# An attention layer on one core: scores and values' products in 64-row halves in one stretch, and the totals of the group norm in the values' bank

## The reference

```python
# group norm: 16 groups along the last axis of x, over (C, H, W/16)
m = mean(g); s = var(g); xn = (g - m) / sqrt(s + 1e-5)
# windows: 8 x 8 pixels, a 4 x 4 grid of windows; m = 64 positions in a window, n = 16 windows
q, k, v = xh @ Wq, xh @ Wk, xh @ Wv            # 224 x 224 each
sim  = einsum('bmhid,bmhjd->bmhij', q2 * scale, k2) + pos_emb   # 8 heads of 28, 16 x 16 scores
attn = softmax(sim, axis=-1)
o    = einsum('bmhij,bmhjd->bmhid', attn, v2)
out  = x + (o @ Wo + bo)
```

## Time and profile before

| | |
|---|---|
| Time, median of 3 runs | 3674.86 us (3674.0 to 3676.15) |
| Profiled execution: time, span | 3674.84 us, 3672.9 us |
| PE busy | 3608.4 us, 98% |
| DVE busy | 3032.9 us, 83% |
| ACT busy | 2940.0 us, 80% |
| POOL busy | 2045.4 us, 56% |
| Granted TensorE clock | 1.0 of full speed |

### The profile page before, as it was taken

The page is one execution under the profiler, slowest core; times in us unless marked ns, Lnnn a source line. Parts: engine busy times, 40 slices in busy tenths (PEclk is TensorE's granted clock), DMA queues, the critical chain, the costliest instruction groups (busy, mean ns, idle before and its releaser), DMA issues.

```text
span 3672.9 us, 167555 instructions
## 1 busy us (share of the span) xinstructions
PE 3608.4 (98%) x67842; PEld 2625.2 (71%) x67842; DVE 3032.9 (83%) x5028; ACT 2940.0 (80%) x5377; POOL 2045.4 (56%) x3334
## 2 busy tenths in 40 slices
PE   5999999999999999999999999999999999999998
PEld 3777777777777777777777777777777777777776
DVE  6888888888888888888888888888888888888876
ACT  6888888888888888888888888888888888888874
POOL 4555555555555555555555555555555555555553
PEclk9999999999999999999999999999999999999999
DMA  4555555555555555555555555555555555555544
GB/s 95 139 144 136 146 144 142 137 145 143 141 138 150 142 137 143 145 143 137 143 146 144 136 145 144 144 134 145 143 145 135 145 142 145 136 146 143 141 126 117
DMA packets 252111, 513.67 MB, mean 140 GB/s; under 512 B 62672, under 2 KB 63120, under 8 KB 251536
## 3 DMA queue, kind: packets, MB, share of 16 engines
q1 hardware_dynamic: 250000, 504.35, 52.4%
q10 hardware_dynamic: 1536, 0.07, 0.0%
HBM read 118.31 MB, written 117.44 MB: 64 GB/s over the span
## 4 chain that ended last, share of the span: by engine, by line
PE 87%; issue 5%; POOL 3%; DVE 2%; ACT 1%; DMA 0%; POOLq 0%; SPq 0%; DVEq 0%; ACTq 0%
PE ps_out L327 18%; PE ps_q L327 16%; PE ps_k L327 16%; PE ps_v L327 14%; PE ps_o L370 13%; PE ps_s L358 10%; POOL sc L724 1%; ACT xn L484 1%; POOL xlo L732 1%; POOL newton L706 1%; DVE part L622 0%; POOL sc L737 0%; PE ps_tot L423 0%; DVE sc L651 0%; DVE pt_f L664 0%
## 5 line engine op out<-in xcount | busy, mean ns | idle before, releaser
L724 POOL TENSOR_TENSOR sc<-sc,mx 128x512 f32<-128x512 f32 x512 | 536.5, 1048 | 876.3 <-DVE mx L658 876.3
L484 ACT ACTIVATE xn<-x_sb,norm_add,norm_mul 112x128 f32<-112x128 f32 x2048 | 1016.7, 599 | 5.0 <-POOL norm_add L717 3.1
L737 POOL TENSOR_TENSOR sc<-sc,rs 128x512 f32<-128x512 f32 x512 | 536.4, 1048 | 421.7 <-DVE rs L678 421.6
L327 PE MATMUL ps_out<-ohi,wo_s 128*112 128x256 f16 x4096 | 720.8, 278 | 3.1 <-DVE x_sb L634 3.1
L646 DVE TENSOR_TENSOR olo<-ps_o,ohi 128x512 f16<-128x512 f32 x512 | 353.8, 691 | 350.0 <-ACT ohi L526 338.8
L511 ACT ACTIVATE sc<-sc 128x512 f32<-128x512 f32 x512 | 323.3, 632 | 396.3 <-POOL sc L724 396.1
L327 PE MATMUL ps_q<-xhi,wqk 112*128 112x512 f16 x2048 | 611.2, 380 | 12.5 <-POOL xlo L732 9.9
L327 PE MATMUL ps_k<-xhi,wqk 112*128 112x512 f16 x2048 | 609.7, 379 | 0.6 <-ACT q_sb L501 0.6
L370 PE MATMUL ps_o<-p_bd,v_sb 128*32 128x128 f32 x16384 | 553.5, 276 | 9.1 <-DMA p_bd<-pt_f 6.6
L327 PE MATMUL ps_v<-wv_s,xhi 112*128 112x224 f16 x4096 | 560.6, 259 | 0.0
L732 POOL TENSOR_TENSOR xlo<-xn,xhi 112x1024 f16<-112x1024 f32 x256 | 547.3, 2138 | 13.1 <-ACT xhi L495 13.1
(11 more groups left out here) (76 smaller groups left out, 5827.6 us busy)
## 6 DMA issues: line engine op xcount, KB each, us to landing
k_bd<-k_cut SPq DMA_DIRECT2D x1024, 128.0 KB
p_bd<-pt_f SPq DMA_DIRECT2D x2048, 64.0 KB, 2.5
x_sb<-in_x SPq DMA_DIRECT2D x256, 448.0 KB, 4.5
out_y<-x_sb SPq DMA_DIRECT2D x256, 448.0 KB, 3.5
k_cut<-in_L_conv_Wq SPq DMA_DIRECT2D x2, 98.0 KB
k_cut<-in_L_conv_Wk SPq DMA_DIRECT2D x2, 98.0 KB
k_cut<-in_L_conv_Wv SPq DMA_DIRECT2D x2, 98.0 KB
pt_f<-in_L_conv_Wo SPq DMA_DIRECT2D x8, 24.5 KB
```

What stands on the lines that cost most here:

```text
L327: last = nc.tensor.matmul(dst, w_parts(a, ch), x_parts(c, ch), start=(n == 0), stop=(n == 3 * chunks - 1))
L484: nc.scalar.activation(xn[:, b % 2, :, c4, :, :, nw].rearrange("p r c q -> p q r c"), x_sb[:, b % XBUFS].rearrange("p ch (nh r w) -> p (ch ...
L724: nc.gpsimd.tensor_tensor(rows, rows, mx[:, t % 2].unsqueeze(2).broadcast_to(by_row), ALU.subtract).then_inc(shifted, 1)
L737: nc.gpsimd.tensor_tensor(rows, rows, rs[:, t % 2].unsqueeze(2).broadcast_to(by_row), ALU.mult).then_inc(probs, 1)
```

## The change

- The values' product is cut in two along its rows. Each half takes 64 rows (two pairs), 64 columns, and writes a bank of its own: `ps_o` gets a second bank, `p_bd` shrinks from four column blocks to two. There are 32 float32 products where there were 16. Each product's 64 columns lie in four strips of 16, 128 columns apart, and ohi and olo read both banks through the new `in_x_order`.
- Score waits and the values' waits stand together before k's last product (`attention_waits`), so scores and values' products follow in one stretch.
- The totals' product goes to 32 free columns of the values' bank `ps_v`, between q and v, one step later than before (`TOT_LEAD` 11, the join keeps its place as `JOIN_LEAD`). The v product of the next step waits for the semaphore `means`.
- ACT copies and scales the totals (`keep_means`) where DVE did; DVE's six remaining operations stand in a row behind the addition to x.

```diff
-LOAD_LEAD, SUM_LEAD, RSQ_LEAD, TOT_LEAD, STAT_LEAD = 15, 14, 13, 12, 11
+LOAD_LEAD, SUM_LEAD, RSQ_LEAD, JOIN_LEAD, TOT_LEAD, STAT_LEAD = 15, 14, 13, 12, 11, 11
-        p_bd = sb("p_bd", [128, 2, PAIRS, UNIT * 32])
+        p_bd = sb("p_bd", [128, 2, 2, UNIT * 32])
-        ps_o = ps("ps_o", [128, UNIT * 32])
-        ps_tot = ps("ps_tot", [128, 2 * G])
+        ps_o = ps("ps_o", [128, 2, 512])
+        ps_tot = ps_v[0:CP, 0, C:C + 2 * G]
         def in_x_order(ap):
-            return ap.rearrange("p (u c n) -> p u n c", u=T2 * HG, n=WIN)
+            return ap.rearrange("p a (c u n) -> p u n (a c)", c=WS // 2, n=WIN)[:, 0:T2 * HG]
...
-                        sp.dma_start(p_bd[pr * 32:pr * 32 + 32, g % 2, pr, :],
+                        sp.dma_start(p_bd[pr * 32:pr * 32 + 32, g % 2, pr % 2, :],
...
+            def total(b, i):
+                if b is None:
+                    return
+                per_image(pe, joined, b, i)
+                per_image(pe, means, b - 1, i)
+                nc.tensor.matmul(ps_tot, ones[0:CP, 0:CP], both[:, b % 2], start=True, stop=True).then_inc(totals, 1)
...
             def weigh_values(g):
                 for t2 in range(T2):
                     for hg in range(HG):
-                        for h in range(HPG):
-                            unit = (((h // 2) * T2 + t2) * HG + hg) * 2 + h % 2
-                            col = (t2 * HG + hg) * 128
-                            last = nc.tensor.matmul(
-                                ps_o[h * 32:h * 32 + 32, col:col + 128].rearrange("p (r j) -> p r j", j=32),
-                                v_sb[:, g % VBUFS, t2, hg * HPG + h, :],
-                                p_bd[:, g % 2, :, unit * 32:unit * 32 + 32], start=True, stop=True)
+                        for half in range(2):
+                            rows = slice(half * 64, half * 64 + 64)
+                            for h in range(HPG):
+                                unit = (((h // 2) * T2 + t2) * HG + hg) * 2 + h % 2
+                                products = ps_o[h * 32:h * 32 + 32, half, :].rearrange("p (c u n) -> p c u n", c=WS // 2, n=WIN)
+                                last = nc.tensor.matmul(
+                                    products[:, :, t2 * HG + hg, :],
+                                    v_sb[rows, g % VBUFS, t2, hg * HPG + h, :],
+                                    p_bd[rows, g % 2, :, unit * 32:unit * 32 + 32], start=True, stop=True)
...
-                def score_waits():
+                def attention_waits():
+                    g = t - PV_LAG
+                    if is_step(g):
+                        probs_placed(pe, g, i)
+                        per_step(pe, v_kept, g, i)
+                        per_step(pe, o_lo, g - 1, i)
...
                     project_qk(u, 0).then_inc(q_done, 1)
                     per_step(pe, v_kept, u - 1, i)
+                    if image_at(t - 1, TOT_LEAD) is not None:
+                        per_image(pe, means, image_at(t - 1, TOT_LEAD), i)
+                    total(image_at(t, TOT_LEAD), i)
                     project_v(u).then_inc(v_done, 1)
                     per_step(pe, k_kept, u - 1, i)
-                    project_qk(u, 1, score_waits).then_inc(k_done, 1)
+                    project_qk(u, 1, attention_waits).then_inc(k_done, 1)
...
+            def keep_means(b, i):
+                if b is None:
+                    return
+                per_image(act, totals, b, i)
+                per_image(act, factors_ready, b - 1, i, 2)
+                wait(act, stats, STAT_OPS * (b - 1) + 2, i, STAT_OPS * XBUFS)
+                nc.scalar.activation(st[:, :], ps_tot, ACT.Copy, scale=1.0 / GROUP_N).then_inc(means, 1)
...
                 if is_step(u):
                     per_step(act, v_done, u, i)
+                keep_means(image_at(t, TOT_LEAD), i)
+                if is_step(u):
                     per_step(act, pv_done, u - VBUFS, i)
...
                 add_out(t - FINAL_LAG, i)
-                stat_op(stat_b, 4, i)
-                stat_op(stat_b, 5, i)
+                for n in range(STAT_OPS):
+                    stat_op(stat_b, n, i)
```

More of the change, by code:

```diff
@@ L152, in build @@
         totals = sem("totals")
+        means = sem("means")
         stats = sem("stats")
@@ L182, in build @@
         final = sem("final")
-        STAT_OPS = 7
+        STAT_OPS = 6
         NEWTON = 3
@@ L394, in step @@
                     per_step(pe, v_kept, u - 1, i)
+                    if image_at(t - 1, TOT_LEAD) is not None:
+                        per_image(pe, means, image_at(t - 1, TOT_LEAD), i)
+                    total(image_at(t, TOT_LEAD), i)
                     project_v(u).then_inc(v_done, 1)
                     per_step(pe, k_kept, u - 1, i)
-                    project_qk(u, 1, score_waits).then_inc(k_done, 1)
+                    project_qk(u, 1, attention_waits).then_inc(k_done, 1)
                 else:
-                    score_waits()
+                    total(image_at(t, TOT_LEAD), i)
+                    attention_waits()
                 if is_step(t + 1):
                     score(t + 1).then_inc(scored, 1)
[L402 to L408, removed]
+                if is_step(t - PV_LAG):
+                    weigh_values(t - PV_LAG).then_inc(pv_done, 1)
                 g = t - OUT_LAG
@@ L418, in step @@
                     last.then_inc(projected, 1)
[L419 to L424, removed]
             def bound_weights():
@@ L436, in _ @@
             pe.wait_ge(zeroed, N_ZEROED)
-            rounds(pe, step, before_11=bound_weights, before_4=weights_split)
+            rounds(pe, step, before_10=bound_weights, before_4=weights_split)
         @block.scalar
@@ L525, in step @@
                     per_step(act, projected, g - 2, i)
-                    nc.scalar.activation(ohi[:, g % 2], in_x_order(ps_o[:, :]), ACT.Copy).then_inc(o_hi, 1)
+                    nc.scalar.activation(ohi[:, g % 2], in_x_order(ps_o[:, :, :]), ACT.Copy).then_inc(o_hi, 1)
             rounds(act, step, before_12=load_positions, before_4=weights_split)
@@ L586, in stat_op @@
                 if n == 0:
-                    per_image(dve, totals, b, i)
+                    per_image(dve, means, b, i)
                     per_image(dve, factors_ready, b - 1, i, 2)
@@ L591, in stat_op @@
                 if n == 0:
-                    ins = nc.vector.tensor_scalar(st[:, :], ps_tot[0:CP, :], 1.0 / GROUP_N, None, ALU.mult)
+                    ins = nc.vector.scalar_tensor_tensor(var[:, :], mean, -1.0, mean, ALU.mult, ALU.mult)
                 elif n == 1:
-                    ins = nc.vector.scalar_tensor_tensor(var[:, :], mean, -1.0, mean, ALU.mult, ALU.mult)
+                    ins = nc.vector.tensor_tensor(var[:, :], var[:, :], msq, ALU.add)
                 elif n == 2:
-                    ins = nc.vector.tensor_tensor(var[:, :], var[:, :], msq, ALU.add)
+                    ins = nc.vector.tensor_scalar(var[:, :], var[:, :], 0.0, EPS, ALU.max, ALU.add)
                 elif n == 3:
-                    ins = nc.vector.tensor_scalar(var[:, :], var[:, :], 0.0, EPS, ALU.max, ALU.add)
+                    ins = nc.vector.tensor_scalar(half_var[:, :], var[:, :], 0.5, None, ALU.mult)
                 elif n == 4:
-                    ins = nc.vector.tensor_scalar(half_var[:, :], var[:, :], 0.5, None, ALU.mult)
-                elif n == 5:
                     ins = nc.vector.tensor_scalar(guess[:, :], var[:, :].bitcast(I32), 1, None, ALU.logical_shift_right)
@@ L640, in step @@
                 stat_b = image_at(t, STAT_LEAD)
-                stat_op(stat_b, 0, i)
                 g = t - OUT_LAG
@@ L644, in step @@
                     per_step(dve, o_hi, g, i)
-                    nc.vector.tensor_tensor(olo[:, g % 2], in_x_order(ps_o[:, :]), ohi[:, g % 2],
+                    nc.vector.tensor_tensor(olo[:, g % 2], in_x_order(ps_o[:, :, :]), ohi[:, g % 2],
                                             ALU.subtract).then_inc(o_lo, 1)
@@ L654, in step @@
                         ALU.mult, ALU.add).then_inc(biased, 1)
-                stat_op(stat_b, 1, i)
                 if is_step(t):
@@ L658, in step @@
                     nc.vector.reduce_max(mx[:, t % 2], rows, axis=AX.X).then_inc(maxed, 1)
-                stat_op(stat_b, 2, i)
                 if is_step(t - 1):
@@ L672, in step @@
                 group_squares(image_at(t, RSQ_LEAD - 1), 1, i)
-                stat_op(stat_b, 6, i)
                 if is_step(t):
@@ L733, in step @@
                         by_channel_half(xlo[:, h % 2]), half_of_xn(h), by_channel_half(xhi[:, h % 2]), ALU.subtract).then_inc(x_lo, 1)
-                join(image_at(t, TOT_LEAD), i)
+                join(image_at(t, JOIN_LEAD), i)
                 if is_step(t):
```

1 line of the change is left out of this document (removed).

## The result

The changed kernel takes 3895.24 us (median of 4 runs, 3890.91 to 3898.6), the kernel before beside it 3674.68 (4 runs, 3674.0 to 3676.15): a ratio of 1.0599, 95% interval 1.0581 to 1.0617. It is 6.0% slower, 220.6 us. The profiled execution took 3898.46 us.

The account below looks back on a forecast made before the run. It took PE and the softmax cycle of VectorE, GpSimd and ScalarE as equally long bounds, so PE's saving gave nothing; 3674.84 us less 3.8 for PE being always ahead, plus 0.5 at the start, gave 3671.5 us, range 3645 to 3705.

Parts of the forecast that it names:

- The two cycles: PE's own steps (168.9 us in 24) and the softmax cycle of VectorE, GpSimd and ScalarE (168.82) run equally long.
- Rival A: PE is the true bound and its whole saving arrives: 3562 us, or 3511; chance 0.08.
- Step (1): Values' product in 64-row halves: 0.79 us instead of 1.01, so 0.22 us less a PE step, perhaps 0.10 more.
- (3): PE's saved 0.22 us a step becomes its wait for VectorE's bias, some 113 us in all; end unchanged.
- Rival B: The values' product gets longer, making PE the longer cycle once over about 1.02 us: 3772 us; chance 0.07.
- (2): Three waits moved to k's last product on PE cost nothing, covered by 1.3 us.
- (4): ohi and olo reading two banks with a stride of 128: taken as 0, at most 0.10 us a turn.
- rival C: Reads of two banks lengthen the softmax cycle: 3726 us at the upper bound, 3700 at half; chance 0.09.
- (5): Totals' product costs PE the same; ScalarE's new copy takes 0.3 us, covered by its idle time before the exponential.
- (6): VectorE's six small statistics in a row: row sum some 0.2 us later, 0.7 us idle left, no effect.
- (7): Start and tail: the totals' copy on ScalarE in the first images' chain costs 0.5 us.
- Rival D: Less overlap with PE shortens the other engines' instructions: 3645 to 3664 us; chance 0.13.

Follow-up runs that it names:

- Experiment 9: The kernel before without the third of v's three passes (8 of 12 products), 0.4 us a step less for PE: 3669.06 us, ratio 0.9986.
- Experiment 1: The changed kernel with the values' products back to 16 of full rows in one bank, all else of the change kept: 3681.89 us, ratio 1.0024.
- shifted kernels: The changed kernel with 24 or 32 small products (96 or 128 instructions) run once ahead of the loop: 3824.65 us and 3860.51 us.
- dense added products: Experiment 1's kernel with 16 or 8 small products a step added between scores and values' products: 3960.05 us and 3803.0 us.
- shifted_128: The changed kernel with 32 small products (128 instructions) run once ahead of the loop: 3860.51 us, ratio 1.0498.
- experiment 2: The changed kernel with the output product moved between the scores and the values' products, same instructions: 3842.84 us, ratio 1.0463.
- pad_in_v: Experiment 1's kernel with 16 small products a step added thinly, 8 ahead of each half of v's products: 4033.59 us, ratio 1.0975.
- pad_in_burst: Experiment 1's kernel with 16 small products a step added between scores and values' products: 3960.05 us, ratio 1.0786.

## Why the prediction was wrong

It said 3671.5 us; it is 3895.24.

- **The two cycles, and that shortening one gives nothing: right.** Experiment 9 took from PE just what this change takes and gained 5.4 us, where the sum had 3.8. Rival A (3562 us) falls with it.
- **Step (1), a size, low.** Foreseen were 0.22 us and perhaps 0.10 for the missing change of shape; the undisturbed step saves 0.39. The pace of the scores held, and the last records of the scores and the first of the values' products even mix in time.
- **The step that failed is (3)**, "the gain turns into a wait of PE for the bias". PE's step is taken there as the sum of its stages. It is 6.60 us only while the instructions come. Where a piece of 256 would be used up in 1.8 to 3.5 us (the time between borders less the gap, for seven of the eight stalled borders in the steps), it stops (the eighth, 8648, comes behind such a piece), and the mean is 7.50: 0.45 above the 7.04 of before, over 488 steps some 220 us, the whole loss. PE waits 0.7 us for the bias in all, where the prediction had some 113. The gaps of over 0.5 us make 301 us, against 1.2 in the kernel before. The rest of the way back from 6.60 to 7.50 is smaller: steps with neither such a gap nor a lowered clock take 6.80 us in the mean, with values' products at 0.80 us in the median from first to last record and the totals' product once in four, and the clock is lower after long stops (below). Even without stalls the wait had the wrong name: in experiment 9 PE's relief goes into waits for xlo and for the addition to x, and 1.3 us into the bias.
- **Rival B named the place and not the mechanism.** "Instructions double in one burst of 128" is the cause, but it was priced by a slower pace in every step (over 1.02 us a stage, 3772 us at its example, chance 0.07). What happened is a normal or better pace with stops of 0.7 to 2.6 us in the median at one border in four. The page before had a hint: the 554 packets of the instruction queue, 16384 bytes each, against PE's records would have given pieces of some 256 instructions. That a piece can come late it did not show.
- **(2), moved waits: right, nearly.** Experiment 1 has them, at 1.0024. **(4): right.** ohi takes 599 ns in both, olo 692 against 691; rival C falls. **(5)**: ScalarE's copy takes 0.20 us, not 0.3, and was covered. **(6)**: nothing to see. **(7)**: the first q starts 0.5 us earlier, not 0.5 later. Rival D: experiment 9 is 0.14% faster, 5.4 us, and not the 11 us at which D began.
- **A reading too general.** The 0.32 us at the back edge was taken for every pass. In the whole run before, PE waited on "issue" ahead of q five times, 2.6 us; most passes have no such gap. The sum of 168.9 us in 24 steps is near the measured mean (24 x 7.044 = 169.1) all the same.

Not settled: what sets the price of the back edge. It is 2.2 us after, 1.7 and 1.6 in the shifted kernels, 2.0 and 2.4 with dense added products, and nothing with thin ones, whose body begins about as far from a border (some 150 instructions) as that of shifted_128. Why some packets start late (behind 8392, 4.7 us after the border) is open too; whether data transfers delay them was not tried.

## What to carry to other kernels

A change that makes an engine's work denser has a second price beside its pace: count the instructions of the stretch and look for the shortest time that 256 consecutive ones would need. Here nothing stalled in the version where that was 4.2 us. Stops of up to 2.9 us in the median came for the most part where it was 1.8 to 3.9 us, at the border of that piece or at the next one; the stretch counts, not the total. And before relieving an engine that is 98% busy, look for a second cycle of the same length: here a relief of the same size was worth 5 us, so the change could hardly win, and it lost 220.

## What the hardware showed beyond that

**Stops that cost twice.** After a long stall the granted clock can be halved for a while. Chain and windows of the changed kernel around one (windows: us, busy of PE, PEld, DVE, ACT and POOL, clock, DMA share, GB/s):

```profile
2042.72 3.27 issue
2045.98 0.67 PE ps_o L382 x27
2046.65 2.74 PE ps_out L330 x12
2049.39 2.56 PE ps_q L330 x6
```

```profile
2045.80:2048.60 2.80, 2.62 (x37) 2.44 (x37) 1.35 (x3) 0.60 (x1) 1.89 (x5) 0.50 0.96 200
2049.00:2051.50 2.50, 2.50 (x8) 1.02 (x7) 2.50 (x4) 0.00 (x0) 1.76 (x5) 0.50 0.42 145
2052.00:2056.00 4.00, 4.00 (x148) 3.01 (x147) 0.94 (x2) 4.00 (x8) 1.10 (x4) 1.00 0.21 49
```

Behind a stop of 3.27 us the clock is at 0.50, the 1.2 GHz level, and back at 1.00, 2.4 GHz, by 2052; the output product takes 2.74 us there where it takes 1.45 in the steps above, and q 2.56 instead of 1.30. The trace has 32 such stretches in the loop, 137 us in all, each with a stop of 1.9 us or more within it or just ahead; the kernel before has none in its loop. Most stops do without: of the 93 gaps of over 1.7 us about a third have such a stretch, and of the 12 of over 3 us nine.

**Moving a loop costs percent.** The same loop, 96 instructions further on in the program, is 71 us (1.8%) faster, and 128 further on 35 us. With a stage this dense, a hundred instructions ahead of the loop that run once change the time by more than the relief of experiment 9 does.

**Changing the tile's shape** costs 0.27 us a step for the one stage moved in experiment 2 (6.60 to 6.87), which is two changes more, and 0.42 for the four more of pad_in_v against pad_in_burst (7.26 to 7.68): 0.10 to 0.13 us a change (estimate), near the 0.10 that the prediction read off the rows.
